# Two transformer layers on one core: the opening from the bit layer on reordered, deferred FFN chunks behind the last projection, and the last batch's end rearranged

## The reference

```python
# L0 "expert" (called q in the kernel): int8 smooth-quant linears, weights are the batch's side inputs
h = smooth_quant_linear(x, guw); gate, up = split(h); y = smooth_quant_linear(silu(gate) * up, ctx)
# L0 ffn (bit layer): ternary weights, 704 hidden units
y = (sigmoid(x @ q(w1).T) * (x @ q(w2).T)) @ q(w3).T      # q(w) = clip(round(w / mean|w|), -1, 1)
# L1 cross attention: 16 heads of 128, 8 key/value heads, keys from ctx (256 rows of 128)
q = x @ Wq; k = ctx @ Wk; v = ctx @ Wv; y = softmax(q k^T / sqrt(128)) v @ Wo
# L1 ffn: a shared expert of 1024 units plus a routed expert of 128 units,
# the routed one scaled by the softmax weights of the two largest of 8 router logits
y = mlp(x, sh_gate, sh_up, sh_down) + w(x @ router.T) * mlp(x, r_gate, r_up, r_down)
```

## Time and profile before

| | us |
|---|---|
| median of 3 timed runs | 407.45 (406.76 to 409.78) |
| profiled execution | 410.09 |
| its span, first to last instruction | 408.3 |
| TensorE busy in the span | 392.5 |
| VectorE, ScalarE, GpSimd busy | 302.1, 229.6, 164.1 |
| mean granted TensorE clock | 0.991 |

### The profile page before, as it was taken

One profiled execution on the slowest core, in us unless ns is written; L12 is line 12 of the kernel. 1 busy time (PEld: TensorE's weight loads), 2 busy tenths in 40 slices (PEclk: granted clock), 3 DMA queues, 4 the chain that ended last, 5 costly groups with the idle time before them and its releaser, 6 DMA issues.

```text
span 408.3 us, 8458 instructions
## 1 busy us (share of the span) xinstructions
PE 392.5 (96%) x3015; PEld 369.6 (91%) x3015; DVE 302.1 (74%) x978; ACT 229.6 (56%) x608; POOL 164.1 (40%) x261
## 2 busy tenths in 40 slices
PE   7898999999999999999999999999999999999896
PEld 6887988998899989999999989998999899999795
DVE  4788888789867889777756989787667866665544
ACT  1896687665643466666543466766444666654231
POOL 2113638774734344335352425235443333332231
PEclk9999999999999999999998999999999999999899
DMA  7999300000000200000000100000000000000000
GB/s 245 328 347 364 83 2 0 3 2 0 3 2 0 82 0 2 2 1 2 2 26 2 56 1 2 2 0 3 2 26 2 0 2 0 2 2 2 26 2 26
DMA packets 15097, 16.86 MB, mean 41 GB/s; under 512 B 1552, under 2 KB 14032, under 8 KB 15056
## 3 DMA queue, kind: packets, MB, share of 16 engines
q1 hardware_dynamic: 15056, 16.33, 12.4%
HBM read 15.28 MB, written 1.05 MB: 40 GB/s over the span
## 4 chain that ended last, share of the span: by engine, by line
PE 79%; DVE 7%; ACT 4%; issue 3%; DMA 3%; POOL 1%; SPq 1%; DVEq 0%; POOLq 0%
PE bank_qa L381 10%; PE bank_u L611 7%; PE bank_pt L597 7%; PE bank_o L628 7%; PE bank_s L577 6%; PE bank_s L381 6%; PE bank_o L632 3%; PE bank_u L615 3%; PE bank_pt L381 3%; PE bank_s L585 3%; PE bank_s L496 3%; DMA wq_raw<-in_wqT 3%; PE bank_u L695 3%; PE bank_x L381 2%; ACT prob L933 2%
## 5 line engine op out<-in xcount | busy, mean ns | idle before, releaser
L1214 POOL TENSOR_SCALAR prob<-prob,row_inv,valid_b 128x256 f32<-128x256 f32 x128 | 71.1, 564 | 94.9 <-DVE row_inv L1570 94.9
L933 ACT ACTIVATE prob<-prob,row_min 128x256 f32<-128x256 f32 x128 | 64.0, 501 | 54.4 <-DVE row_min L1562 54.2
L1575 DVE TENSOR_TENSOR pt_lo<-bank_pt,pt_hi 128x512 fp32r<-128x512 f32 x64 | 43.7, 682 | 16.1 <-ACT pt_hi L893 16.0
L1562 DVE CUSTOM_DVE_ANT_0 prob<-bank_s,masked 128x256 f32<-128x256 f32 x128 | 48.8, 419 | 1.7 <-PE bank_s L585 1.1
L597 PE MATMUL bank_pt<-ident,prob 128*128 128x128 f32 x256 | 42.4, 278 | 1.7 <-DVE c_lo L1774 1.0
L1225 POOL TENSOR_TENSOR act_lo<-act_raw,act_hi 128x256 fp32r<-128x256 f32 x32 | 24.1, 753 | 49.5 <-ACT act_hi L996 49.4
L893 ACT ACTIVATE pt_hi<-bank_pt 128x512 fp32r<-128x512 f32 x64 | 37.5, 586 | 8.3 <-PE bank_pt L597 8.0
L1581 DVE TENSOR_TENSOR ut_lo<-bank_u,ut_hi 128x512 fp32r<-128x512 f32 (+1 forms) x36 | 22.7, 632 | 24.3 <-ACT ut_hi L893 23.8
L381 PE MATMUL bank_qa<-xt_hi,a_hi 128*128 128x256 f32 x126 | 39.4, 313 | 0.3 <-DVE qa_lo L1543 0.3
L597 PEld LDWEIGHTS bank_pt<-ident,prob 128*128 128x128 f32 x256 | 29.4, 141 | 9.5 <-POOL prob L1214 4.4
L381 PE MATMUL bank_qa<-xt_lo,a_hi 128*128 128x256 f32 x126 | 35.2, 280 | 0.0
(11 more groups left out here) (319 smaller groups left out, 1232.4 us busy)
## 6 DMA issues: line engine op xcount, KB each, us to landing
wq_raw<-in_wqT SPq DMA_DIRECT2D x4, 512.0 KB, 7.8
wo_raw<-in_wo SPq DMA_DIRECT2D x4, 512.0 KB, 8.2
w_raw<-in_w12T SPq DMA_DIRECT2D x2, 704.0 KB, 7.7
gate_raw<-in_gateT SPq DMA_DIRECT2D x2, 576.0 KB, 7.7
up_raw<-in_upT SPq DMA_DIRECT2D x2, 576.0 KB, 9.5
down_raw<-in_downT SPq DMA_DIRECT2D x2, 576.0 KB, 11.3
x<-in_x SPq DMA_DIRECT2D x4, 256.0 KB, 6.3
guT<-in_guT SPq DMA_DIRECT2D x4, 256.0 KB, 3.8
```

Source lines behind the costliest of these rows:

```text
L933: act.activation(row, row, ACT.Exp, scale=-1.0, bias=row_min[:, h % 2, t:t + 1], accum_out=row_sum[:, h % 2, t:t + 1]).then_inc(S["s_exp"], 1)
L1214: pool.tensor_scalar(row, row, row_inv[:, h % 2, t:t + 1], valid_b[:, 0:1], ALU.mult, ALU.mult).then_inc(S["s_norm"], 1)
L1562: dve.tensor_tensor_reduce(out=prob[:, h % 2, t, :], in0=src[:, t * T:(t + 1) * T], in1=masked[:, :], scale=1.0, scalar=3.0e38, op0=ALU.ad ...
L1575: dve.tensor_tensor(pt_lo[:, :, cols], bank["pt"][:, :].rearrange("p (s t) -> p s t", s=2), f32(pt_hi[:, :, cols]), ALU.subtract).then_inc ...
```

## The change

Six edits are made together.

1. The bit layer of batch 0 is written out: four ups, then downs and ups in turn; folded unit 7 stands behind down 3, unit 8 behind the layer; nine `keep_busy` transposes in it are gone. New waits hold a product slot until its low part and its down product are done. ScalarE makes the splits and copies in another order, GpSimd makes the low part of the context of batch 0 (VectorE did), and VectorE has `lnq_apply(1)` between the statistics and `ln_apply` of the attention's layer norm.
2. Folded units 12 to 15 each come one place later on TensorE, units 13 and 15 in other banks; four more `keep_busy` transposes are gone; the low parts of units 13 to 15 are made beside heads 0 and 1; `turn_probs(0, 0)` waits for 13 of them and not for 16. ScalarE splits two more FFN units beside heads 5 and 6, GpSimd one fewer.
3. The row of mask addends is made on ScalarE; VectorE only finds whether a batch has a valid column.
4. The router's logits are made with the router's weights loaded and 256 tokens streamed, copied to SBUF by ScalarE and turned back by two transposes, a chunk later; `route_top` and `route_sum` come one chunk later.
5. Of batch 2's deferred chunks two now stand behind `project(3, 15)`, in banks pt and qa, and the downs of both behind `ffn_turn`.
6. In batch 3 the routed chunk is the sixth of nine; it is added ahead of the last chunk's product, and the shared sum is added and stored in two halves.

The core of the diff:

```diff
+FOLDED_LATE = {0: (13, 14), 1: (15,)}
...
-LATE_BANKS = (("qa",), ("qa",), ("x0", "qa"), ("qa",))
-LATE_UP = ({(12, 1): 0, (14, 0): 1},) * 2 + ({(11, 1): 0, (12, 1): 1, (14, 0): 2},)
-LATE_DOWN = ({(15, 0): 0},) * 2 + ({(13, 1): 0, (14, 1): 1},)
-LATE_SIG = ({13: 0, 15: 1},) * 2 + ({12: 0, 13: 1, 14: 2},)
-LATE_HIGH = ({14: 0},) * 2 + ({13: 0, 14: 1, 15: 2},)
+LATE_BANKS = (("qa", "qa"), ("qa", "qa"), ("x0", "qa", "pt", "qa"), ())
+LATE_UP = ({(12, 1): 0, (14, 0): 1},) * 2 + ({(12, 1): 0, (14, 0): 1},)
+LATE_DOWN = ({(15, 0): 0},) * 2 + ({(14, 1): 0},)
+LATE_SIG = ({13: 0, 15: 1},) * 2 + ({13: 0, 14: 1},)
+LATE_HIGH = ({14: 0},) * 2 + ({14: 0, 15: 1},)
 FFN_LOADS = 6
 FFN_UNITS = 2 * FFN_LOADS
-FFN_HI_HEADS = (0, 1, 2, 4)
+FFN_HI_HEADS = (0, 1, 2, 4, 5, 6)
 FFN_HI_EARLY = FFN_UNITS - len(FFN_HI_HEADS)
-FFN_LO_HEADS = (0, 1, 2, 4, 5, 6, 7, 8)
+FFN_LO_HEADS = (1, 2, 4, 5, 6, 7, 8)
...
+        def routed_at(b):
+            return at_once(b) - (4 if b == NB - 1 else 1)
+
         def ffn_chunk(b, p):
-            n = at_once(b)
-            return FFN_CHUNKS - 1 if p == n - 1 else p if p < n else p - 1
+            return FFN_CHUNKS - 1 if p == routed_at(b) else p if p < routed_at(b) else p - 1
...
-        PREP_BANKS = ("qa", "o", "s0", "qa", "o", "u", "x1", "qa", "o", "x1", "qa", "s1", "pt", "o", "x1", "pt")
+        PREP_BANKS = ("qa", "o", "s0", "qa", "o", "u", "x1", "qa", "o", "x1", "qa", "s1", "pt", "u", "x1", "o")
...
-            store(NB - 1)
-            sp.wait_ge(S["out_done"], 16 * NB)
+            for t in range(NT):
+                sp.wait_ge(S["ffn_x"], NB + t)
+                sp.dma_start(out[NB - 1, t * P:(t + 1) * P], x[:, NB - 1, t, :]).then_inc(S["out_done"], 16)
+            sp.wait_ge(S["out_done"], 16 * (NB - 1 + NT))
...
             def turn_probs(b, h):
                 if b == 0 and h == 0:
-                    pe.wait_ge(S["prep_lo"], 16)
+                    pe.wait_ge(S["prep_lo"], PREP_BANKS.index("pt") + 1)
...
+                else:
+                    pe.wait_ge(S["prep_lo"], PREP_BANKS.index("u", 6) + 1)
...
             def route(b):
                 pe.wait_ge(S["router_hi"], 1)
                 pe.wait_ge(S["router_lo"], 1)
-                for t in range(NT):
-                    for k in range(ND):
-                        cols = slice(t * P, (t + 1) * P)
-                        last = split_mm(bank["x1"][:, t * NR:(t + 1) * NR], yt_hi[:, k, cols], yt_lo[:, k, cols],
-                                        router_hi[:, k, :], router_lo[:, k, :], k == 0, k == ND - 1)
+                for k in range(ND):
+                    last = split_mm(bank["x1"][0:NR, 0:T], router_hi[:, k, :], router_lo[:, k, :],
+                                    yt_hi[:, k, :], yt_lo[:, k, :], k == 0, k == ND - 1)
                 last.then_inc(S["route_mm"], 1)
+
+            def route_turn(b):
+                pe.wait_ge(S["route_copy"], b + 1)
+                for t in range(NT):
+                    last = pe.transpose(bank["x1"][:, t * NR:(t + 1) * NR], logits[0:NR, t * P:(t + 1) * P],
+                                        ident[0:NR, 0:NR])
+                last.then_inc(S["route_t"], 1)
...
+                    if c == (ROUTE_LATE + 1 if last else 1):
+                        route_turn(b)
...
-                    ffn_down(b - 1, FFN_CHUNKS - 2)
+                    ffn_down(b - 1, FFN_CHUNKS - 3)
...
+                    ffn_up(b - 1, FFN_CHUNKS - 2)
                     ffn_up(b - 1, FFN_CHUNKS - 1)
                     ffn_turn(b)
+                    ffn_down(b - 1, FFN_CHUNKS - 2)
...
-            def beside_bit(c):
-                if c == 2:
-                    prep_unit(7)
-                elif c == 5:
-                    prep_unit(8)
-
-            bit_layer(0, beside_bit)
+            bit_up(0, 0)
+            bit_up(0, 1)
+            bit_up(0, 2)
+            bit_up(0, 3)
+            bit_down(0, 0)
+            bit_up(0, 4)
+            bit_down(0, 1)
+            bit_up(0, 5)
+            bit_down(0, 2)
+            bit_down(0, 3)
+            prep_unit(7)
+            bit_down(0, 4)
+            bit_down(0, 5)
+            prep_unit(8)
             prep_unit(9)
             prep_unit(10)
             prep_unit(11)
-            prep_unit(12)
             keep_busy(3, "s0")
             att_turn(0)
-            prep_unit(13)
+            prep_unit(12)
...
+            prep_unit(13)
             prep_unit(14)
             prep_unit(15)
-            keep_busy(4, "u")
...
+            def mask_row(b):
+                act.wait_ge(S["mask_in"], 16 * (b + 1))
+                if b > 0:
+                    act.wait_ge(S["s_min"], NT * H * b)
+                act.activation(masked[:, :], mask8[:, :], ACT.Copy, scale=-MASKED, bias=MASKED
+                               ).then_inc(S["mask_row"], 1)
...
                 act.wait_ge(S["bit_prod"], BIT_CHUNKS * b + c + 1)
+                if b == 0 and c >= 3:
+                    act.wait_ge(S["bit_y"], c - 2)
...
+                    if p == (ROUTE_LATE if last else 0):
+                        act.wait_ge(S["route_mm"], b + 1)
+                        act.copy(logits[:, :], bank["x1"][0:NR, 0:T]).then_inc(S["route_copy"], 1)
...
+            pool.wait_ge(S["ctx_hi"], 1)
+            pool.tensor_tensor(cx_lo[:, :, :], cx[:, :, :], f32(cx_hi[:, :, :]), ALU.subtract)
+            pool.tensor_tensor(cxT_lo[:, :], cxT[:, :], f32(cxT_hi[:, :]), ALU.subtract).then_inc(S["ctx_lo"], 1)
...
+                if b == 0 and c >= 3:
+                    dve.wait_ge(S["bit_lo"], c - 2)
...
+            def last_residual(b):
+                dve.wait_ge(S["ffn_y"], FFN_CHUNKS * (b + 1))
+                dve.wait_ge(S["routed_x"], b + 1)
+                for t in range(NT):
+                    dve.tensor_tensor(x[:, b, t, :], bank["u"][:, t * D:(t + 1) * D], x[:, b, t, :], ALU.add
+                                      ).then_inc(S["ffn_x"], 1)
...
+                    if b == 0 and h in FOLDED_LATE:
+                        for k in FOLDED_LATE[h]:
+                            prep_lo(k)
...
+                    if last and p == n - 1:
+                        routed_residual(b)
...
-            for c in range(BIT_CHUNKS):
-                bit_act(0, c)
-                if c == 0:
-                    prep_lo(6)
-                elif c == 1:
-                    dve.wait_ge(S["x1_in"], 16)
-                    link(lnq_stats_of([1]))
-                    lnq_variances([1])
-                elif c == 2:
-                    mask_row(0)
-                    prep_lo(7)
-                elif c == 3:
-                    q_weight_scales(1)
-                elif c == 4:
-                    ctx_split_lo(0)
-            lnq_apply(1)
+            bit_act(0, 0)
+            bit_act(0, 1)
+            prep_lo(6)
+            bit_act(0, 2)
+            bit_act(0, 3)
+            dve.wait_ge(S["x1_in"], 16)
+            lnq_stats_of([1]).then_inc(S["x1_stats"], 1)
+            bit_act(0, 4)
+            dve.wait_ge(S["x1_stats"], 1)
+            lnq_variances([1])
+            bit_act(0, 5)
+            q_weight_scales(1)
+            prep_lo(7)
             bit_residual(0)
             ln_stats_of(0, "lna")
             prep_lo(8)
+            lnq_apply(1)
             ln_apply(0, "lna")
             prep_lo(9)
             prep_lo(10)
             ln_lo(0, "lna", xt_hi, xt_lo)
             prep_lo(11)
-            prep_lo(12)
             first_queries_lo(0)
             first_queries_lo(1)
+            valid_batch(0)
             row_minima(0, 0)
             row_minima(0, 1)
-            prep_lo(13)
+            prep_lo(12)
...
-            prep_lo(14)
-            prep_lo(15)
```

More of the change, by code:

```diff
@@ L523, in bit_turn, with bit_layer @@
                 turn_xn(b, "lnb", bank["x0"]).then_inc(S["lnb_t"], 1)
-            def bit_layer(b, between=None, begun=0):
-                for c in range(begun, BIT_CHUNKS + 2):
+            def bit_layer(b, between):
+                for c in range(3, BIT_CHUNKS + 2):
                     if c < BIT_CHUNKS:
                         bit_up(b, c)
-                    if begun == 0 and c >= BIT_CHUNKS:
-                        keep_busy(*((3, "s1"), (6, "pt"))[c - BIT_CHUNKS])
-                    if c >= 2:
-                        bit_down(b, c - 2)
-                    if between is not None:
-                        between(c)
+                    bit_down(b, c - 2)
+                    between(c)
             def att_turn(b):
@@ L695, in ffn_down @@
                         pe.matmul(dst[:, t * D:(t + 1) * D], act_hi[:, p % 3, t * P:(t + 1) * P], half[:, c, :],
-                                  start=(t == 0 and half is down_hi and p in (0, n - 1, n)), stop=False,
+                                  start=(t == 0 and half is down_hi and p in (0, routed_at(b), n)), stop=False,
                                   skip_group_check=True)
@@ L1150, in _ @@
             exps(0, 1)
+            prep_hi(13)
             prep_hi(14)
             prep_hi(15)
```

(4 more changed lines are left out.)

133 lines of the change are left out of this document (78 added, 55 removed).

## The result

The changed kernel takes 402.68 us (median of 4 executions, 402.59 to 402.94) against 407.38 (4, 406.76 to 409.78): ratio 0.9869, 95% interval 0.9839 to 0.9899. That is 1.3% faster, inside the range of the prediction and 0.5 us above its value. The profiled execution took 402.94 us, its span is 401.2.

The account below looks back on a forecast made before the run. TensorE's instruction issue was taken as the bound; 2.4 + 1.3 + 0.7 + 0.2 = 4.6 us of order and 0.7 of clock, 5.3 us, gave 402.1 from the 407.45 median, 402.6 from the profiled time; forecast 402.2 us, range 399.4 to 405.6.

Parts of the forecast that it names:

- the order sum, 4.6 us: Whole kernel: gains from opening, router, last batch and end, 2.4 + 1.3 + 0.7 + 0.2 us, without the clock.
- The bound: Whole kernel: issue-bound on TensorE, busy 96% of the span; work moved from a full stage into a hole gains its length.
- (a): Whole kernel: the forecast itself holds, 400.7 to 403.3 us; chance 0.52.
- (e): Opening, 42 to 60 us: fillers held the clock; without them it falls and stays down, 412 us; chance 0.04.
- The opening, 2.4 us: Bit layer of batch 0 to head 0's turn: new order and removed fillers save 2.4 us, bounds 0.8 and 3.4.
- rival (b): Opening: VectorE gives the gain back, the opening yields only 0.8 us, time 404.4 us; chance 0.24.
- Router, 1.3 us: Router of each batch: six 256-column matmuls and two transposes save 0.33 us, four times 1.3 us, bounds -1 and 1.8.
- (d): Batch ends: the router's round trip is exposed, 1 us each, saving turns to -2.7, time 406.5 us; chance 0.07.
- Last batch, 0.7 us: Behind the last projection: two deferred ups fill the wait before the turn, 0.7 us of order, bounds 0 and 1.5.
- Clock, 0.7 us: Half-clock falls at batch 1's router and behind the last projection: fewer falls give 0.7 us, bounds -1.5 and 2.9.
- Rival (c): Clock: the median too had two falls and both go, time 400.0 us; chance 0.13.
- End, 0.2 us: Final store: first half issued under the second addition, last half 0.1 us earlier; 0.2 us, bounds 0 and 0.8.

Follow-up runs that it names:

- e11: The kernel before without the thirteen filler transposes of the opening, its order kept; ratio 0.9989 to the kernel before.
- e10: The changed kernel with thirteen filler transposes put back into the bit layer of batch 0; ratio 0.9893 to the kernel before.
- e12: The changed kernel with the mask row made on VectorE again, in batch 0 beside the first turns; ratio 0.9882 to the kernel before.
- e1: The kernel before with the new opening alone, the mask row on VectorE beside the first turns; ratio 0.9965 to the kernel before.
- e2: The kernel before with the new router alone; ratio 0.9966 to the kernel before.
- e6: The changed kernel with the routed sum made behind the third product instead of the fourth; ratio 0.9850 to the kernel before.
- e7: The changed kernel with the routed sum earlier and ScalarE's mask row of the next batch one chunk earlier; ratio 0.9850 to the kernel before.
- e3: The kernel before with the deferred chunks alone, two ups between the last projection and the turn; ratio 0.9961 to the kernel before.
- e9: The kernel before with sixteen identity transposes in the 2.00 us idle time ahead of the last batch's ffn_turn; ratio 0.9972 to the kernel before.
- e8: The changed kernel with the old router of twelve 8-column matmuls; ratio 0.9913 to the kernel before.
- e4: The kernel before with the new end alone, routed chunk sixth and the sum stored in two halves; ratio 0.9988 to the kernel before.

## Why the prediction was right, step by step

**In short.** The mechanism was right, and the order sum, 4.6 us, came out at 4.6, but by errors that cancel: 0.2 too little for the opening, 0.1 for the last batch and 0.3 for the end, against 0.62 lost at the passage to batch 3 that no term held. The 0.5 us by which the result misses the value is the clock term. That the total lies so close is in part luck.

**The bound.** Right: TensorE's issue time sets the pace, and each gain arrived as such. All four parts went the way forecast, (a) held, (e) did not occur.

**The opening, 2.4 us.** Measured 2.55 at head 0's turn and 2.6 at batch 0's ffn_turn. The residual (44.1 forecast, 44.25), the layer-norm turn (1.8 us earlier, 1.96) and head 0's turn (57 to 57.6, 57.08) were right. Two things in the working were wrong or missing. First, 0.99 us was counted for nine fillers and 0.5 for four; e11 shows that taking them out gives 0.0, since idle time takes their place. It is the order that makes room, and the fillers then have to go, because they would cost 1.4 (e10). Second, the mask row's move was costed at nothing. For the sum that held, since the kernel before made the row in 0.28 us inside the bit layer; what I didn't see is that beside the first turns it costs the kernel 0.9 us (e12). With the row there the opening gains 1.8 us (e1), so rival (b), which had it at 0.8, would have been right in part; with edit 3 it had nothing.

**Router, 1.3 us.** The size was right, 0.33 per batch (e2), six matmuls 0.69 and two transposes 0.22 us; no round trip was exposed, so (d) fell. (Its four exposed trips, -2.7 us, lay outside the term's own lower bound of -1.) What the step missed is "a chunk later": the forecast looked at who waits for ScalarE and not at what VectorE does next, and 0.4 to 0.5 us of the 1.3 went there (e2, e6). With 0.14 for the mask row (e7) that is the 0.62 us of the passage.

**Last batch, 0.7 us.** 2.1 before the turn and 1.3 paid behind it, 0.8 (e3). Idle 0.56, forecast 0.6; 7.9 us behind the projection, forecast 7.7.

**Clock, 0.7 us.** As a mean the term was right: 0.86 stretches an execution before and 0.2 after, at 1.15 us each, are 0.76. In the four executions that the forecast was measured against it gave next to nothing. Their median is 407.38; three of them, 406.76, 407.31 and 407.45, lie where executions without a stretch lie (407.61 in the table; their own clocks are not on record), so as far as these times tell the median had no stretch to give back, and the 4.7 us of the result are order alone. Over the 65 executions the median is 408.62, and against that the changed kernel's 402.87 is 5.75 us less, 1.0 of them clock. The price of a fall was over-estimated too: 1.5 us at the router in the profile, as counted, but 1.1 and not 1.4 behind the projection (e9). "A matter of luck whose occasion the change removes" is borne out for both places, each by a run that alters it alone (e8 the router, e9 the hole), on six and twelve executions. Rival (c) would have needed a median with two stretches; 13 of 65 executions have them. The rule of the Trainium skill (TensorE: Matmul & The Clock Gate, "Part 1: The HAM clock gate") agrees with e9 in its direction: with transposes of the identity in the idle time there were fewer stretches. "Explained" was too strong a word in the prediction, since the same idle time doesn't always bring the fall (rows below). That removing fillers speaks against the change is not borne out (e10, e11), nor does the rule by itself account for the router, where the profile has TensorE busy in every microsecond (e8). Why twelve 8-column matmuls bring the clock down in some executions is open.

The turn behind the last projection in the profiles of e1 and e4, with the idle time of the kernel before and, at 0.76 us where the half clock made it 1.08, at full clock:

```profile
378.49 0.76 PE L391 MATMUL bank_x<-ident,hs 128*128 128x128 f32 x4 [2.00 <-DVE hs L1357]
...
380.22 0.76 PE L394 MATMUL bank_x<-ident,hs 128*128 128x128 f32 x4 [2.00 <-DVE hs L1347]
```

**End, 0.2 us.** 0.5 (e4): the term was mis-sized because the saving in the half store's landing was taken close to its lower bound of nothing. It landed in 1.8 us, 0.4 less. The Trainium skill (DMA: Bandwidth & Descriptors, "Anatomy of one DMA") gave about 0.3 less as an estimate; the difference agrees, though both landings lie below the 2.3 and 2.6 us that its formula gives. The section fits that formula to DMAs issued by GpSimd, and these stores are issued by SyncE, which the prediction left unsaid.

The parts at full clock, from the profiles: 2.6 (opening, with edit 3) + 1.3 + 0.8 + 0.5 - 0.6 (the passage) = 4.6 us; from the layer's first row to the end it is 371.5 (e9, whose order is that of the kernel before) against 366.9 and 367.2, 4.3 to 4.6.

## What to carry to other kernels

A filler or a wait inside a stretch that waits anyway costs nothing and its removal gives nothing; price it by what ends the wait behind it. When a step moves one place along a stream, look at what stands next on that engine and at what the neighbour engine is doing in that instant, not at the step's own wait alone. Where the time comes in discrete steps from the clock, sort executions by granted clock first and compare like with like; differences of 1 us then show in ten executions, as long as the kernel before runs beside them (it drifted by 1.0 us from one group of runs to the next), and smaller ones in the profiles' stages.

## What the runs showed of the hardware

Some VectorE instructions last until a GpSimd instruction that started just before them has ended: `cxT_lo` (two inputs in SBUF) took 0.96 instead of 0.42 us, `masked` 1.55 instead of 0.28, both started 0.02 to 0.14 us behind a GpSimd subtraction and ended 0.14 to 0.29 us behind its end. All fifteen cxT_lo that started behind it, in five profiles, took 0.96; started 0.26 to 0.27 us ahead of it (e6, e7, the kernel before) they took 0.42. Not every pair does this. In the changed kernel an instruction with one input in a PSUM bank ran at its usual 0.42 us inside GpSimd's 0.86, and the kernel before made `masked` in 0.28 us while a 128x2 instruction of GpSimd was running:

```profile
303.28 0.42 DVE L1662 SCALAR_TENSOR_TENSOR sig<-sig,bank_pt 128x256 f32<-128x256 f32 x1
...
303.05 0.86 POOL L1274 TENSOR_TENSOR act_lo<-act_raw,act_hi 128x256 fp32r<-128x256 f32 x1 [0.51 <-ACT act_hi L1032]
...
39.42 0.28 DVE L1538 TENSOR_SCALAR masked<-mask 128x256 f32<-128x256 uint8 x1
...
38.93 0.81 POOL L1185 TENSOR_TENSOR lnq_rstd<-lnq_rstd,half_exp 128x2 f32<-128x2 f32 x1
```

The Trainium skill (SBUF — State Buffer, "Who interferes with whom") states such stops as an exclusive lock that goes to whichever starts first. The rows of cxT_lo agree, and so does that of `masked` in e12; why `masked` wasn't stopped at 39.42 us is open. The prediction hadn't used the section; with it the 0.96 us of cxT_lo could have been foreseen.

TensorE's clock stood at half for some 3.4 us at three places, in none of them in every execution: while the weights come in (e2), behind a busy router of 8-column matmuls, and behind 2.00 us of idle time. With both later occasions removed, 5 stretches were left in 30 executions (the changed kernel, e6, e7, e10, e12); with the old router alone left, 15 in 28 (e3, e8, e9: 6 in 10, 6 in 6 and 3 in 12, a scatter that stays open); with the idle time alone left, 6 in 10 (e2).
